# Half of each cell's hidden state on GpSimd, history products in single passes, a semaphore for each sum, and a new order on every engine of a recurrent kernel

## The reference

```python
encoded = tanh(xt @ We + st @ Ue + be)
new_state = tanh(einsum('bd,cds->bcs', xt, Wx) + einsum('bs,cst->bct', st, Ws) + bk)
mem = concatenate([concatenate([encoded, err])[:, None, :], mem[:, :-1, :]], axis=1)
a = relu(mem.reshape(b, -1) @ enc_w1 + enc_b1)
agent_in = relu(a @ enc_w2 + enc_b2)
h1, c1 = lstm_cell(agent_in, h1, c1, ...)
h2, c2 = lstm_cell(h1, h2, c2, ...)
gate = softmax(h2 @ gate_w + gate_b)
theta = clamp01(mean(abs(mem[:, :10, -1])) * 2.5)
gate = gate * theta + gs * (1 - theta)
st = einsum('bc,bcs->bs', gate, new_state)
pred = clamp01(st[:, -1]);  err = pred - yt
```

## Time and profile before

| | us |
|---|---|
| median of 3 runs (range) | 5656.6 (5656.21 to 5656.87) |
| span of the profiled execution | 5654.1 |
| TensorE busy | 5444.6 (96%) |
| VectorE busy | 4678.1 (83%) |
| ScalarE busy | 3830.9 (68%) |
| GpSimd busy | 1646.7 (29%) |
| share of the chain that ended last: TensorE, ScalarE, VectorE | 69%, 15%, 12% |

### The profile page before, as it was taken

One profiled execution on the slowest core, in us unless ns is written; L12 is line 12 of the kernel. 1 busy time (PEld: TensorE's weight loads), 2 busy tenths in 40 slices (PEclk: granted clock), 3 DMA queues, 4 the chain that ended last, 5 costly groups with the idle time before them and its releaser, 6 DMA issues.

```text
span 5654.1 us, 184300 instructions
## 1 busy us (share of the span) xinstructions
PE 5444.6 (96%) x67584; PEld 3397.7 (60%) x67584; DVE 4678.1 (83%) x12841; ACT 3830.9 (68%) x9217; POOL 1646.7 (29%) x3589
## 2 busy tenths in 40 slices
PE   7999999999999999999999999999999999999998
PEld 4666666666666666666666666666666666666665
DVE  7888888888888888888888888888888888888887
ACT  5666666666666666666666666666666666666665
POOL 2222222222222222222222222222222222222222
PEclk9999999999999999999999999999999999999999
DMA  2111111111111111111111111111111111111111
GB/s 66 28 29 30 28 31 28 31 28 31 28 31 28 31 28 28 31 28 31 28 31 28 31 28 31 28 29 30 28 31 28 31 28 31 28 31 28 31 28 39
DMA packets 299286, 172.38 MB, mean 30 GB/s; under 512 B 156734, under 2 KB 263882, under 8 KB 298714
## 3 DMA queue, kind: packets, MB, share of 16 engines
q1 hardware_dynamic: 293568, 159.42, 10.8%
q10 hardware_dynamic: 5146, 3.66, 0.2%
HBM read 74.65 MB, written 2.10 MB: 14 GB/s over the span
## 4 chain that ended last, share of the span: by engine, by line
PE 69%; ACT 15%; DVE 12%; issue 4%; DMA 0%; POOL 0%; ACTq 0%; POOLq 0%; DVEq 0%
PE chain L412 17%; PE a_ps L374 10%; PE cand_ps L343 8%; PE cand_ps L334 8%; ACT a_sb L523 6%; PE chain L399 6%; PE a_ps L363 6%; ACT gates L548 5%; DVE cell_in L708 5%; DVE added L694 4%; PE chain L308 4%; PE a_ps L385 4%; PE chain L429 4%; PE cand_ps L329 3%; ACT tanh_c L554 3%
## 5 line engine op out<-in xcount | busy, mean ns | idle before, releaser
L363 PE MATMUL a_ps<-hist,w_hist 125*64 125x512 f16 x12288 | 1700.2, 381 | 24.9 <-DMA w_hist<-enc_table 24.9
L785 DVE TENSOR_REDUCE state<-mixed 128x64 f32<-128x512 f32 x2048 | 1352.6, 681 | 34.1 <-POOL mixed L873 0.7
L541 ACT ACTIVATE cand<-cand_ps 128x512 f32<-128x512 f32 x2048 | 1154.6, 590 | 184.8 <-PE cand_ps L343 184.8
L412 PE MATMUL chain<-cell_in,cell_w 128*64 128x128 f32 x16384 | 1092.8, 276 | 0.7 <-ACT cell_in L531 0.5
L412 PEld LDWEIGHTS chain<-cell_in,cell_w 128*64 128x64 f32 x16384 | 888.3, 136 | 288.2 <-ACT cell_in L531 181.5
L900 POOL TENSOR_TENSOR err_ring<-pred_now,ys 128x8 f32 x512 | 128.6, 251 | 3106.0 <-DVE pred_now L792 3106.0
L548 ACT ACTIVATE gates<-chain 128x512 f32<-128x512 f32 x1024 | 611.4, 597 | 619.8 <-PE chain L412 619.8
L363 PEld LDWEIGHTS a_ps<-hist,w_hist 125*64 125x64 f16 x12288 | 658.6, 110 | 447.2 <-issue 26.0
L554 ACT ACTIVATE tanh_c<-gates 128x128 f32<-128x128 f32 x1024 | 316.7, 309 | 690.0 <-DVE gates L700 690.0
L694 DVE SCALAR_TENSOR_TENSOR added<-gates 128x256 f32<-128x256 f32 x1024 | 435.5, 425 | 419.4 <-ACT gates L548 419.4
L708 DVE SCALAR_TENSOR_TENSOR cell_in<-gates,tanh_c 64x128 f32<-64x128 f32 x2048 | 588.0, 287 | 159.4 <-ACT tanh_c L554 145.6
(11 more groups left out here) (74 smaller groups left out, 6660.7 us busy)
## 6 DMA issues: line engine op xcount, KB each, us to landing
x_sb<-in_x_l SPq DMA_DIRECT2D x260, 256.0 KB, 2.8
hist<-entry_parts SPq DMA_DIRECT2D x2048, 25.0 KB
w_hist<-enc_table SPq DMA_DIRECT2D x258, 128.0 KB, 2.4
y_rows<-in_y_l SPq DMA_DIRECT2D x260, 8.0 KB
ys<-in_y ACTq DMA_DIRECT2D x1, 2048.0 KB, 16.3
preds_out<-preds SPq DMA_DIRECT2D x1, 2048.0 KB, 8.1
cand<-in_encoder ACTq DMA_DIRECT2D x1, 640.0 KB, 3.8
cell_w<-in_cell ACTq DMA_DIRECT2D x2, 256.0 KB, 4.8
```

What stands on the lines that cost most here:

```text
L363: nc.tensor.matmul(a_ps[g][ENC * half:ENC * half + ENC, :], w_hist[0:HROWS, w_slot(u), kk, wp, :], hist[0:HROWS, xp, k, at:at + 512], star ...
L412: last = nc.tensor.matmul(chain[g][rows, P * r:P * r + P], cell_w[c][:, hf, r, :], cell_in[c][:, g, hf, :], start=False, stop=True, skip_g ...
L541: ins = nc.scalar.activation(cand[:, g, q // 2, :, q % 2, :, :].rearrange("p h s c -> p h (s c)"), cand_ps[q][:, :].rearrange("p (h k) -> ...
L785: V.tensor_reduce(state[:, g, hf, 2 * pair:2 * pair + 2, :], mixed[:, pair, hf, :, :, :], AX, ALU.add)\
```

## The change

- `new_hidden` is split: VectorE forms one half of 64 rows of each cell's h (one instruction in place of two), GpSimd the other half. GpSimd needs two instructions for its half, `out_gate_low` (output gate plus one, as soon as the gates are there) and `new_hidden` (times tanh_c). Cell 1, the logits and next_hidden wait for both engines' counts.
- `history` can issue single passes, and the passes of blocks 0 to 2 are spread between other steps.
- The candidates' bias products are a step of their own (`candidates_bias`) ahead of encoder2.
- `q_sum` becomes four semaphores (half by pair) in place of two, so a wait can name the sums that it needs; `q_cand` starts at one.
- Every engine's `phase` has a new order. TensorE's, between two encoder2: encoder2(A), candidates_x(A), cell 0, candidates_s(A), three passes of B (blocks 0, 0, 1), bias of cell 1, encoded_x(B), one pass, cell 1, one pass, transposes(B), two passes, encoded_s(B), one pass, block 3, logit bias, logits(A), encoder1_now(B), one pass of C, bias of cell 0 (B), candidates_bias(B).
- `mix_quarter` runs in the same phase as the gate, ahead of `keep_prediction`; `mix(.., 0)` and three of the four sums stand in the next phase.

The diff, cut to its core (the indent is shortened; of the four `phase` functions only the new order is shown, the old one is above):

```diff
 TENSOR_HEAD = 0
-SUMS = 2
 ENTRY_ROWS = (slice(0, HALF), slice(HALF, ER))
 HIST_INC = 16 * Q
-CAND_ORDER = (2, 1, 3, 0)
-MIX_ORDER = (1, 0)
+CAND_ORDER = (1, 2, 3, 0)
...
+        out_gate = [sb(f"out_gate{n}", [P, GROUPS, P]) for n in range(2)]
...
     g, n, u = item
-    pe.wait_ge(q_sum[hf], SUMS * n)
+    for pair in range(2):
...
-def encoded_x(item, before, extra):
+def encoded_x(item, extra):
     g, n, u = item
     x_wait(item, extra)
-    if before:
-
-        for pair in MIX_ORDER:
-            pe.wait_ge(q_mul[pair], before[1] + GROUPS if pair == MIX_ORDER[1] else before[1])
+    for pair in range(2):
+        pe.wait_ge(q_mul[pair], n)
     for rows in ENTRY_ROWS:
...
-    g, n, u = item
-    if before:
-        for q in CAND_ORDER:
-            pe.wait_ge(q_cand[q], before[1])
+def candidates_bias(item):
+    g, n, u = item
+    for q in CAND_ORDER:
+        pe.wait_ge(q_cand[q], n)
     for q in range(Q):
         rows = slice(D_IN * q, D_IN * q + D_IN)
         nc.tensor.matmul(cand_ps[q][:, :], ones16[rows, :], cand_bias[rows, :],
                          start=True, stop=False, skip_group_check=True)
+
+def candidates_x(item):
...
     g, n, u = item
...
-    if before:
-        pe.wait_ge(q_in, before[1])
-
-def history(item, kk):
+
+def history(item, kk, first=0, end=len(PIECES)):
     g, n, u = item
     k = HT - 1 - kk
-    for t, (wp, xp) in enumerate(((0, 0), (1, 0), (0, 1))):
+    for t in range(first, end):
+        wp, xp = PIECES[t]
         for half in range(2):
             at = GB * g + 512 * half
...
         pe.wait_ge(q_h[0], n)
+        pe.wait_ge(q_h_pool[0], n)
...
     pe.wait_ge(q_h[1], n)
+    pe.wait_ge(q_h_pool[1], n)
...
     new, cur, old = items
+    if old:
+        bias_of_cell(old, 0)
+        candidates_bias(old)
+        encoder2(old)
+        candidates_x(old)
+        cell_gates(old, 0)
+        candidates_s(old)
+    if cur:
+        history(cur, 0, 1, 3)
+        history(cur, 1, 0, 1)
+    if old:
+        bias_of_cell(old, 1)
+    if cur:
+        encoded_x(cur, extra)
+        history(cur, 1, 1, 2)
+    if old:
+        cell_gates(old, 1)
+    if cur:
+        history(cur, 1, 2, 3)
+        state_transpose(cur, 0)
+        state_transpose(cur, 1)
+        history(cur, 2, 0, 2)
+        history(cur, 2, 2, 3)
+        history(cur, 3)
     if old:
         logit_bias(old)
         gate_logits(old)
     if cur:
         encoder1_now(cur)
     if new:
+        history_waits(new, extra)
+        history(new, 0, 0, 1)
...
+def agent_input(item, hf):
+    g, n, u = item
+    rows = AGENT_ROWS[hf]
...
     g, n, u = item
     if q == CAND_ORDER[0]:
         act.wait_ge(q_candps, n)
-        act.wait_ge(q_mul[MIX_ORDER[1]], n)
-        act.wait_ge(q_mulpool, n)
+    if q // 2 == 1:
+        act.wait_ge(q_mul[1], n)
+    elif q == 0:
+        act.wait_ge(q_mul[0], n)
+    else:
+        act.wait_ge(q_mulpool[1], n)
...
+def next_hidden(item, hf):
+    g, n, u = item
+    rows = CELL0_OUT[hf]
+    act.wait_ge(q_h_pool[0] if hf == POOL_HALF[0] else q_h[0], n)
+    last = nc.scalar.activation(cell_in[0][rows, g, hf, :], cell_in[1][rows, g, hf, :], ACT.Copy)
+    if hf == POOL_HALF[0]:
+        last.then_inc(q_hnext, 1)
...
     new, cur, old = items
     if cur:
         cell_tanhs(cur, 1)
     if new:
         state_take(new)
     if cur:
+        next_hidden(cur, 1)
         value_tanh(cur, 1)
     if new:
         at_least_zero(new)
         encoded(new)
+        candidates(cur, 0)
         exponentials(cur)
     if new:
         encoder1(new)
+        entry_high(new)
+        agent_input(new, 0)
+        agent_input(new, 1)
+        cell_tanhs(new, 0)
+    if cur:
+        next_hidden(cur, 0)
+    if new:
+        candidates(new, 1)
+        value_tanh(new, 0)
+        candidates(new, 2)
+        candidates(new, 3)
...
+def new_hidden(item, c, hf):
+    g, n, u = item
+    rows = (CELL0_OUT, CELL1_OUT)[c][hf]
     dve.wait_ge(q_tanhc[c], n)
-    for hf in range(HF):
-        rows = (CELL0_OUT, CELL1_OUT)[c][hf]
-        last = V.scalar_tensor_tensor(cell_in[1][rows, g, hf, :], gates[c][rows, g, 0, :], 1.0,
-                                      tanh_c[c][rows, g, :], ALU.add, ALU.mult)
+    last = V.scalar_tensor_tensor(cell_in[1][rows, g, hf, :], gates[c][rows, g, 0, :], 1.0,
+                                  tanh_c[c][rows, g, :], ALU.add, ALU.mult)
     last.then_inc(q_h[c], 1)
...
 def mix(item, pair):
     g, n, u = item
-    if pair == MIX_ORDER[0]:
-        dve.wait_ge(q_gate, n)
+    dve.wait_ge(q_gate, n)
     if pair == 1:
-        dve.wait_ge(q_cand[2], n)
-        dve.wait_ge(q_cand[3], n)
+        dve.wait_ge(q_cand[2], n + 1)
+        dve.wait_ge(q_cand[3], n + 1)
...
-        dve.wait_ge(q_cand[0], n)
+        dve.wait_ge(q_cand[0], n + 1)
...
 def mix_sum(item, hf, pair):
     g, n, u = item
-    dve.wait_ge(q_mul[pair], n + GROUPS if pair == MIX_ORDER[1] else n)
+    dve.wait_ge(q_mul[pair], n + GROUPS)
     if pair == 0:
-        dve.wait_ge(q_mulpool, n + GROUPS)
+        dve.wait_ge(q_mulpool[1], n + GROUPS)
     V.tensor_reduce(state[:, g, hf, 2 * pair:2 * pair + 2, :], mixed[:, pair, hf, :, :, :], AX, ALU.add)\
-        .then_inc(q_sum[hf], 1)
+        .then_inc(q_sum[hf][pair], 1)
...
     new, cur, old = items
+    if old:
+        mix(old, 0)
+    if cur:
+        cell_terms(cur, 0)
+        cell_value(cur, 0)
+    if old:
+        mix_sum(old, 0, 0)
+    if cur:
+        new_hidden(cur, 0, 1)
         mix_sum(old, 0, 1)
-    if cur:
+        prediction(old)
+    if cur:
         cell_terms(cur, 1)
         cell_value(cur, 1)
+    if new:
+        error_sum(new)
+    if cur:
+        new_hidden(cur, 1, 0)
     if new:
         errors(new, extra)
     if cur:
         peaks(cur)
         below_peak(cur)
+    if new:
+        thetas(new)
+    if cur:
         totals(cur)
         reciprocals(cur)
         shares(cur)
         fresh_gate(cur)
         new_gate(cur)
         mix(cur, 1)
-        mix(cur, 0)
+        mix_sum(cur, 1, 1)
...
+    pool.wait_ge(q_cand[q], n + 1)
     for hf in range(HF):
-        pool.wait_ge(q_sum[hf], SUMS * n + SUMS * (GROUPS - 1))
-    over_s = gate[:, g, 1:Q:2, :].rearrange("p h (o c) -> p h o c", o=1)\
+        pool.wait_ge(q_sum[hf][0], n + (GROUPS - 1))
+    over_s = gate[:, g, q:Q:2, :].rearrange("p h (o c) -> p h o c", o=1)\
         .to_broadcast([P, HF, S, C])
-    G.tensor_tensor(mixed[:, 0, :, 1, :, :], cand[:, g, 0, :, 1, :, :], over_s, ALU.mult)\
-        .then_inc(q_mulpool, 1)
+    G.tensor_tensor(mixed[:, 0, :, q, :, :], cand[:, g, 0, :, q, :, :], over_s, ALU.mult)\
+        .then_inc(q_mulpool[q], 1)
+
+def out_gate_low(item, c):
+    g, n, u = item
+    rows = (CELL0_OUT, CELL1_OUT)[c][POOL_HALF[c]]
+    pool.wait_ge(q_gates[c], n)
+    G.tensor_tensor(out_gate[c][rows, g, :], gates[c][rows, g, 0, :],
+                    ones[rows, 0:1].to_broadcast([HALF, P]), ALU.add).then_inc(q_out[c], 1)
+
+def new_hidden(item, c, hf):
+    rows = (CELL0_OUT, CELL1_OUT)[c][hf]
+    pool.wait_ge(q_out[c], n)
+    pool.wait_ge(q_tanhc[c], n)
+    G.tensor_tensor(cell_in[1][rows, g, hf, :], out_gate[c][rows, g, :], tanh_c[c][rows, g, :],
+                    ALU.mult).then_inc(q_h_pool[c], 1)
...
+    pool.wait_ge(q_pred, n)
     pred = pred_now[:, g, :].rearrange("p (j o) -> p j o", o=1)
     G.tensor_copy(preds[:, tiles, bass.ds(step, 1)], pred).then_inc(q_predout, 1)
...
     new, cur, old = items
+    if cur:
+        kept_share(cur)
+        new_hidden(cur, 0, 0)
+        kept_gate(cur)
+        out_gate_low(cur, 1)
     if old:
         new_error(old, extra)
+    if cur:
+        new_hidden(cur, 1, 1)
     if new:
         entry_low(new)
     if cur:
         gate_in_sbuf(cur)
+        mix_quarter(cur, 1)
+    if old:
+        keep_prediction(old, extra)
+    if new:
+        out_gate_low(new, 0)
```

More of the change, by code:

```diff
@@ L136, in recurrent_kernel @@
                                     "inps", "in", "candps"))
-        q_keptfrom, q_mulpool = (sem(f"q_{n}") for n in ("keptfrom", "mulpool"))
+        q_keptfrom = sem("q_keptfrom")
+        q_mulpool = [sem(f"q_mulpool{q}") for q in range(2)]
         q_cand = [sem(f"q_cand{q}") for q in range(Q)]
@@ L147, in recurrent_kernel @@
                                     "ring", "predout"))
-        q_sum = [sem(f"q_sum{hf}") for hf in range(HF)]
+        q_sum = [[sem(f"q_sum{hf}_{pair}") for pair in range(2)] for hf in range(HF)]
+        q_h_pool = [sem(f"q_h_pool{c}") for c in range(2)]
+        q_out = [sem(f"q_out{c}") for c in range(2)]
         block = ctx.enter_context(nc.Block())
@@ L346, in candidates_s, with history_waits @@
                 last.then_inc(q_candps, 1)
-            def history_waits(item, before, extra):
+            def history_waits(item, extra):
                 g, n, u = item
@@ L524, in encoder1 @@
                     .then_inc(q_a, 1)
[L526 removed]
+            def agent_input(item, hf):
                 g, n, u = item
[L528 to L533 removed]
```

(41 more changed lines are left out.)

61 lines of the change are left out of this document (6 added, 55 removed).

## The result

The changed kernel takes 5758.4 us (median; 5758.1 to 5759.5) against 5656.5: a ratio of 1.018, 95% interval 1.0166 to 1.0195. It is slower, where I forecast 5557 us and gave slower 0.20. The range ended at 5700.

What follows compares the result with a forecast made beforehand. TensorE was taken as the bound: its products 10.59, plus 0.12 and 0.04 lost at joints, gave 10.75 us an item against 10.944, saving 99 us, so 5557.5 us. The 8-in-10 range was 5450 to 5700.

Steps and rivals of the forecast that it cites:

- the forecast's losses at the joints: Waits for h from GpSimd and VectorE holding each other up: 0.12 us at cell 0's joint, 0.04 at cell 1's.
- The price of a shape change: On TensorE, each change of the shape in which the array is divided was taken to cost 0.12 us.
- The count of eight: Shape changes in one item of TensorE's new order: eight, two more than before, adding 0.24 us.
- This joint is met or missed by 0.05, and nothing is left over: h of cell 0 ready at about 5.6 us; cell 1 due at 5.82, its weights loaded some 0.2 ahead.
- The 0.12 of waiting: Ahead of encoder1_now: errors(B) coming earlier would remove this wait, and the product's length would fall from 1.10 to 0.86.
- The last sentence of the prediction: A missed joint put at zero could cost a 0.2 start-up each time: cell 1, the logits, the second transpose.
- The wait at encoder2: While a_sb forms (0.76 us), one pass and two biases (0.78) cover TensorE's wait, put at about 0.13 before.
- Rival (c): GpSimd's queue becomes the loop: 11.14 us an item, 5757 us, slower; chance 0.17.
- Rival (b): Whole-operation blocking between VectorE and GpSimd: 0.25 at cell 0, 0.1 more at cell 1; 5614 to 5680 us; chance 0.18.
- Rival (d): On TensorE each fine piece brings a bubble: 10.83, with joints 10.99 us an item, 5680 us; chance 0.04.
- the list of gains: TensorE's item as a difference: 0.12 + 0.06 + 0.13 waits, 0.24 start-up, 0.06 cell 0, less 0.24 shapes; given as 0.35 less.

Runs made afterwards that it cites:

- s1: The kernel before with one move, the bias of cell 1 between candidates_x and candidates_s, cutting the candidates in two: 5829.7 us, ratio 1.0305.
- t1: The changed kernel with the third pass of history block 2 moved ahead of encoded_s: 5759.0 us, ratio 1.0182.
- v7: v3 with a history pass between logits and encoder1_now and the bias of cell 0 ahead of encoder2: 5692.3 us, ratio 1.0062.
- o4: The changed kernel with TensorE's order of before, cell 0's tanh first, and the single-pass and bias moves of v7: 5703.5 us, ratio 1.0082.
- h2: The changed kernel with all of h on VectorE, GpSimd's four new operations gone: 5730.3 us, ratio 1.0129.
- v3: The kernel before with GpSimd's half of h for cell 1 only, new_error behind it in GpSimd's queue: 5614.9 us, ratio 0.9927.

## Why the prediction was wrong

I had the right bound, the right item length of before, and a sum over TensorE's order. It fails in the size of its terms. Forecast and measured, us an item (measured from the chain of the changed kernel; the forecast's losses at the joints are put where it had them):

| step | forecast | measured |
|---|---|---|
| a_sb and encoder2 | 1.19 | 1.21 |
| candidates_x | 0.98 | 1.07 |
| cell 0 | 1.03 | 1.02 |
| candidates_s | 0.98 | 1.08 |
| three passes, bias, encoded_x, one pass | 1.64 | 1.66 |
| cell 1 | 0.91 + 0.12 | 1.09 |
| pass, transposes, two passes | 1.25 | 1.14 |
| encoded_s | 0.43 | 0.57 |
| four passes, logit bias | 0.90 | 0.89 |
| logits | 0.42 + 0.04 | 0.45 |
| encoder1_now | 0.86 | 0.95 |
| sum | 10.75 | 11.13 |

- **The price of a shape change.** "I take 0.12 for each change of shape" is the step that failed. The count of eight was right; in front of the float32 candidates it is 0.21, as s1 shows in the kernel before with nothing else changed. That is 0.19 an item, 97 us and half of the miss of 201. Before, the float16 bias stood first and paid 0.12; the change moves it away and leaves float32 products at the front, twice. A rule taken from places that all have one property was carried to places without it. At cell 0, where float32 products follow a change too, the 0.12 held (1.02 against 1.03).
- **"This joint is met or missed by 0.05, and nothing is left over" (cell 1).** Met in kind, mis-sized: VectorE's h of cell 0 was held for 0.26, where I had 0.12 in all. Cell 1 took 1.09, behind 0.02 of issue, in place of 1.03. out_gate_low was also sized too low, at 0.42: it takes 0.63, and GpSimd got 1129 us of work in place of 860.
- **encoded_s, which I did not treat as a joint at all.** Two passes stand between transposes and encoded_s where three stood. state_take comes behind the gates of cell 1 on ScalarE, and encoded_s starts late: +0.14. The last sentence of the prediction named a start-up at a missed joint, but for three others. Mending it alone gives nothing, as t1 showed, for the way through GpSimd's h is as long.
- **encoder1_now.** The 0.12 of waiting did go, as forecast. The length fell from 1.10 to 0.95, not to 0.86: in every run in which it stands directly behind the logits without a wait it has 0.95 or 0.96 in most items, and behind a pass of history 0.88 (v7, o4), so 0.1 of start-up belongs to this place.
- **The wait at encoder2** was covered as forecast (0.78 against 0.76). The transposes were 0.11 shorter than forecast, which hid part of the miss.
- **Rival (c)** gave 5757 us and slower, but by GpSimd's queue as the loop, and that isn't what happened: GpSimd's entry_low alone waited 1370 us for ScalarE. The number fits by accident. Rival (b)'s mechanism is the real one at cell 0 (0.26 held, where it had 0.25); all of GpSimd's half is worth 0.12 an item at cell 1, and 28 us when what it gives back is taken off (h2). Rival (d), bubbles at single passes, is not what happened: every lone pass of the changed kernel took 0.22.
- **A slip in the list of gains.** The wait at encoder2 is 0.76 - 0.65 = 0.11 by the earlier trace rows, not 0.13, and the list adds up to 0.37 and not 0.35. The sum over the steps doesn't use it.

The gain I saw exists: 0.27 an item at encoder1_now (0.12 + 1.10 to 0.95). Against it stand 0.19 at cell 1 (0.91 to 1.09 and the short wait), 0.21 between cell 1 and the logits (3016.91 to 3019.33 in the earlier trace rows, 2.42, against 2.63), 0.02 at a_sb, and 0.05 between encoder2 and cell 1, where the extra shape changes and one more pass ate what moving two bias products out of this stretch had freed. The balance, 0.47 - 0.27, is the 0.2 that was measured.

What stays open: why the lost lead of the first load costs 0.12 in one place and up to 0.21 in another. The candidates, encoded_x, cell 0 and the float16 products differ in type, in shape and in the size of their loads at once, and no run separates these. Nor is it shown by a run of its own what cell 1 would take with its h in time; that share is read from the traces.

## What to carry to other kernels

Count the changes of TensorE's tile shape in an order and price each by what stands first behind it; group products of one shape, and put a cheap float16 one first where the products behind it would pay more (0.12 against 0.21 at the candidates). Before moving half of an operation to GpSimd, ask whether VectorE works on two SBUF inputs at that moment: where both start together, the half takes about as long as the whole. Count a slower handing over too (0.1 in v3). The half pays only where something queued behind it on VectorE was the late one (v3). When the chain of waits says 98% TensorE, compare the length of each product with its twin elsewhere: the waits may be inside.

## What the runs showed of the hardware

A change of tile shape costs 0.12 us before float16 products, and before float32 ones 0.12 (cell 0), 0.15 (encoded_x) or 0.21 (candidates); the first load then starts together with the first product (3005.87 in s1) and no longer 0.21 ahead of it. GpSimd's multiply of 64x128 float32 takes 0.45 us when nothing holds it (estimate in the prediction: 0.42), and 0.49 behind VectorE's h; the add with a broadcast column, starting beside terms, 0.63. An order on one engine can't be judged alone: the same order of TensorE gave 6175 or 5638 us, by the place of one tanh on ScalarE.
